# The recurrence of a three-layer kernel: waits taken bank by bank, and another order of its wide products and its sums of returned rows

## The chip, the cores and the metric
The kernel runs on one core of a Trainium2 chip, in one launch. The metric is the device time of the launch in microseconds; the median of three runs counts.

## What is computed
The input x has 4 sequences of 1024 tokens with 256 channels, in fp32. Four layers follow, each on the layer norm of x and added to x: a retention layer, a mixture of experts (8 experts, 2 for each token), the recurrence, and the same experts again. Only the recurrence is touched:
```python
sx = concat([0, x[:, :-1]]) - x                     # the token before, less this one
m = tanh((x + sx * maa_x) @ tm_w1).reshape(B, T, 5, 32)
mix = maa_wkvrg + einsum('btfa,fac->btfc', m, tm_w2)
xw, xk, xv, xr, xg = [x + sx * mix[:, :, i] for i in range(5)]
r, k, v, g = xr @ Wr, xk @ Wk, xv @ Wv, silu(xg @ Wg)
w = exp(-exp(time_decay + tanh(xw @ td_w1) @ td_w2))
# per head of 16 channels, over the tokens, with a = outer(k_t, v_t):
y_t = r_t @ (state + u * a);  state = w_t * state + a
yn = (y - mean(y)) * rsqrt(var(y) + eps) * ln_w + ln_b          # per head
out = (yn * g) @ Wo
```

## The kernel before
Each layer is a block of programs, one for each engine, written out instruction by instruction with semaphores between them; nothing plans the order but these lists. In the recurrence channels lie on the partitions (two halves, kt = 0 and 1) and tokens along the columns. The 4096 tokens are cut into 8 chunks of 512 (n = 0 to 7), two for each sequence. Every engine runs a loop over n that interleaves three chunks: `now` is chunk n, `ahead` chunk n + 1, whose mixes, decays, keys and receptances are made, and `behind` chunk n - 1, whose y is normalised, gated and multiplied with Wo.

Inside a chunk the recurrence is done by blocks of 64 tokens. r and k are multiplied by products of the decays over 2, 4, 8, 16, 32 and 64 tokens (`chain`, 25 steps on DVE); TensorE makes the scores within blocks (`scores_by_4`, `_16`, `_32` for each of four groups i of 128 tokens), DVE masks them (`mask`), `additions` makes what each block of 64 adds to the state, a scan on DVE carries the state (`states`), and `outputs(n, i)` sums scores times v and r times state into y. Near tokens (within 4) are done apart (`near_0`, `near_1_sum`, `near_23_sum`).

PSUM is nearly full: `core` (4 banks) holds scores, y and the additions, and two pairs of banks, `even` and `odd`, are used by all else in turn. So most waits in TensorE's list say that a bank has been read. `mix_scaled` counts DVE's ten mixes of a chunk in the order W_1, W_0, V_0, V_1, K_0, R_0, K_1, R_1, G_0, G_1; each reads one bank of `even` or `odd`. GpSimd then adds x to each (`add_token`, `mix_ready`). `log_ready` counts ACT's logarithm of the variance, which lies in `even`. `hidden_ready` counts two Tanh on ACT that follow the `hiddens` products.

The layer before this one, the experts, leaves its results in DRAM (`y_rows`). For chunk n + 2 they come back by DMA in two tiles, and `add_ys(n + 2, part)` adds them to x on DVE, two instructions for each of four parts; parts 2 and 3 are of the second tile. After part 3 the tiles are free for the next DMA. `stats_of_x` and `moments_of_x` make the statistics of the sum, ACT's `norm` normalises it, and `transpose_x` puts it into `even`.

The lines that matter in the profile: L1909 norm, L1923 tokens, L1930 and L1931 hidden_out, L1942 decay_of, L1949 and L1953 copies of k and r, L1957 copy of v, L1972 silu, L1985 log, L2018 parted copies of r, L2056 y_raw; L2139 is every `linear` (hiddens, hidden_decay, keys, receptances, gate), L2155 deltas, L2188 deltas_g, L2202 decays, L2259 near_0, L2264 near_1_sum and near_23_sum, L2306, L2319 and L2330 the scores by 4, 16 and 32, L2343 transpose_k, L2357 additions, L2378 and L2385 outputs, L2398 variance, L2413 output; L2538 the products of r, L2635 mix, L2671 mask, L2687 the scan, L2738 add_ys; L1833 add_token, L1866 sum_y.

Of the kernel before, what the change touches and what calls it, by code (L numbers as in the profile page):

```python
# [6 lines left out]
ACT = mybir.ActivationFunctionType  # L7
# [6 lines left out]
KT = C // P  # L14
# [1571 lines left out]
CHUNKS = B * CPB  # L1586


def recurrence(nc, held, semaphores, used, d, x, x_stats, y_rows, home, weight, rec_loaded, first_rows, name="rec"):
    with ExitStack() as ctx:  # L1590
# [201 lines left out]
        with nc.Block() as block:  # L1792
# [109 lines left out]
            def _(act):  # L1902
# [80 lines left out]
                def log(c):  # L1983
                    act.wait_ge(var_in_psum, c + 1)
                    act.activation(square[:], even[:], ACT.Ln, bias=eps[:]).then_inc(log_ready, 1)  # L1985

                def root(c):
                    act.wait_ge(log_ready, c + 1)
                    act.activation(square[:], square[:], ACT.Exp, scale=-0.5).then_inc(y_rstd_ready, 1)
# [69 lines left out]
                for n in range(-2, CHUNKS + 1):  # L2059
                    now, ahead, behind = 0 <= n < CHUNKS, 0 <= n + 1 < CHUNKS, n >= 1  # L2060
                    if behind:
                        y_raw(n - 1, 2)
                    if now:
                        k_out(n)
                    if ahead:
# [55 lines left out]
            def _(pe):  # L2121
# [63 lines left out]
                def deltas_g(c):  # L2185
                    pe.wait_ge(hidden_d_ready, c + 1)
                    for kt in range(KT):
                        mm = pe.matmul(odd[:, kt, :], tm_w2_g[LORA * kt:LORA * (kt + 1), kt * P:(kt + 1) * P],  # L2188
                                       hidden_g[LORA * kt:LORA * (kt + 1), :], start=True, stop=True)
                    mm.then_inc(delta_in_psum, 1)  # L2190

                def hidden_decay(c):
                    pe.wait_ge(mix_ready, c * MIXES + W_0)
                    pe.wait_ge(mix_scaled, c * MIXES + R_0)
                    linear(odd[:, 0, :], td_w1, mixed["w"], slice(0, P)).then_inc(d_in_psum, 1)

                def decays(c):
                    pe.wait_ge(hidden_d_ready, c + 1)
                    pe.wait_ge(mix_scaled, c * MIXES + R_1)
                    for kt in range(KT):  # L2200
                        own = slice(kt * LORA_D, (kt + 1) * LORA_D)
                        mm = pe.matmul(even[:, kt, :], td_w2[own, kt * P:(kt + 1) * P], hidden_d[own, :], start=True, stop=True)  # L2202
                    mm.then_inc(decay_in_psum, 1)
# [48 lines left out]
                def near_0(c):  # L2252
                    pe.wait_ge(chain, c * CHAIN + NEAR_0B)
                    if c >= 1:
                        pe.wait_ge(log_ready, c)
                    else:
                        pe.wait_ge(xnt_ready, min(2, CHUNKS))
                    for kt in range(KT):
                        mm = pe.matmul(even[:, kt, :], same_head[:], y_near[:, kt, :], start=True, stop=True)  # L2259
                    mm.then_inc(near_in_psum, 1)  # L2260
# [73 lines left out]
                def transpose_k(c):  # L2334
                    pe.wait_ge(chain, c * CHAIN + K64B)
                    pe.wait_ge(k_copied, c * COPIES + K64_REST)
                    if c + 1 < CHUNKS:
                        pe.wait_ge(mix_scaled, (c + 1) * MIXES + V_0)
                    else:
                        pe.wait_ge(x_added, c)  # L2340
                    for i in range(CT):
                        for kt in range(KT):
                            mm = pe.transpose(even[:, i // 2, i % 2 * C + kt * P:i % 2 * C + (kt + 1) * P],  # L2343
                                              k_64[:, kt, i * P:(i + 1) * P], ident[:])
                    mm.then_inc(k_rows_in_psum, 1)
# [43 lines left out]
                def variance(c):  # L2389
# [7 lines left out]
                    for kt in range(KT):  # L2397
                        mm = pe.matmul(even[:, kt, :], mean_m[:], square[:, kt, :], start=True, stop=True)  # L2398
                    mm.then_inc(var_in_psum, 1)

                def output(c):
# [7 lines left out]
                    else:  # L2409
                        pe.wait_ge(log_ready, c + 1)  # L2410
                    for i in range(CT):
# [13 lines left out]
                for n in range(-2, CHUNKS + 1):  # L2425
# [44 lines left out]
                    if now:  # L2470
                        scores_by_4(n, 3)
                        scores_by_16(n, 3)
                        scores_by_32(n, 3)
                        outputs(n, 1)
                    if ahead:
                        keys(n + 1, 0)
                    if now:
                        outputs(n, 2)
                    if ahead:
                        keys(n + 1, 1)  # L2480
                    if now:
                        outputs(n, 3)
                    if ahead:
                        receptances(n + 1)
                    if now:
                        gate(n, 0)
                        gate(n, 1)
# [4 lines left out]
            def _(dve):  # L2492
# [296 lines left out]
                for n in range(-1, CHUNKS + 1):  # L2789
# [49 lines left out]
                    if now:  # L2839
                        decay_product(n, 32)  # L2840
                        r_to_64(n)
                    if ahead:
                        mix_kr(n + 1, 0)
                    if now:
                        mask(n, 1)
                        states(n)
                    if then:
                        add_ys(n + 2, 2)
                    if ahead:
# [174 lines left out]
```

## Time and profile before

| | us |
|---|---|
| median of 3 runs | 1347.71 |
| lowest, highest | 1342.36, 1349.99 |
| profiled execution, its own time | 1351.96 |
| its span | 1350.1 |
| recurrence, first to last of its instructions in the span | about 555 to 1075 |
| one steady chunk | 58.6 |
| TensorE busy in 59 us of a steady chunk | 54.7 |

An engine's busy time leaves out its waits, so in a chunk of 58.6 us the rest of TensorE's time is waits. A row of the timeline has start, duration, engine, line, operation, out<-in, the count that was merged, and in brackets how long the engine had been idle before it and what released it; "issue" means that nothing in the profile did. Instructions of one engine overlap a little, so a duration reaches into the next row.

### The profile page before, as it was taken

What the parts mean: (1) busy time and instruction counts of PE and PEld (TensorE: products, weight loads), DVE (VectorE), ACT (ScalarE), POOL (GpSimd) and SP (SyncE); (2) the same over time, 40 slices, a digit from 0 to 9 for tenths busy, and PEclk for the clock granted to TensorE, in tenths of its full rate; (3) what the DMA queues carried; (4) which work ended last, traced back from release to release, by engine and by line L of the source; (5) the groups of instructions that cost most, each with busy time, mean ns of one, the idle gap of its engine ahead of it and who ended that gap; (6) DMA issues with size and microseconds to landing.
All of it is one profiled execution on the core that took longest, in us unless ns stands there. A gap on an engine that the chain in (4) does not pass through costs nothing. (4 is left out here: it accounts for less than half of the span.)

```text
span 1350.1 us, 34954 instructions
## 1 busy us (share of the span) xinstructions
PE 1148.6 (85%) x14041; PEld 818.7 (61%) x14041; DVE 927.6 (69%) x1959; ACT 612.8 (45%) x1310; POOL 551.3 (41%) x537
## 2 busy tenths in 40 slices
PE   7999999975699999478999999899987648999970
PEld 4677777763588888235555555555555436888850
DVE  6778787757765655568778797877854376656546
ACT  3344343413355555153736456374653233555534
POOL 3333233202377776325162341516321105777750
PEclk9999999988799999698999999999997679999995
DMA  8132222009643332200000101000000195333338
GB/s 305 55 109 95 88 93 86 35 1 346 209 170 104 104 102 89 72 32 3 33 3 33 33 3 33 4 32 4 2 2 3 33 387 159 104 103 103 105 108 336
DMA packets 50682, 125.66 MB, mean 93 GB/s; under 512 B 7648, under 2 KB 26976, under 8 KB 47712
## 3 DMA queue, kind: packets, MB, share of 16 engines
q1 hardware_dynamic: 36896, 86.20, 17.8%
q0 software_dynamic: 13632, 37.24, 8.8%
q8 instruction: 117, 1.92, 0.6%
q14 instruction: 37, 0.30, 0.1%
HBM read 79.63 MB, written 43.78 MB: 91 GB/s over the span
## 5 line engine op out<-in xcount | busy, mean ns | idle before, releaser
L1090 POOL DMA_INDIRECT ffn_xs<-xn_rows,ffn_from_row x142 | 137.7, 969 | 123.0 <-DVE ffn_second_y_at L1472 80.4
L1098 POOL DMA_INDIRECT y_rows<-ffn_ys,ffn_to_row x142 | 140.2, 987 | 54.9 <-issue 35.2
L1253 PE MATMUL ffn_ps_h<-ffn_w_high,ffn_xst 128*128 x568 | 155.1, 395 | 0.7 <-issue 0.7
L1500 DVE TENSOR_TENSOR ffn_act_in<-ffn_silu_g,ffn_ps_h 128x256 f32<-128x256 f32 x142 | 59.9, 422 | 139.1 <-ACT ffn_silu_g L1132 139.1
L1132 ACT ACTIVATE ffn_silu_g<-ffn_ps_h 128x256 f32<-128x256 f32 x142 | 54.8, 386 | 144.3 <-PE ffn_ps_h L1253 144.3
L1273 PE MATMUL ffn_ps_o<-ffn_w,ffn_act_t 128*128 x284 | 117.2, 435 | 0.5 <-DVE ffn_act_t L1505 0.5
L1253 PEld LDWEIGHTS ffn_ps_h<-ffn_w_high,ffn_xst 128*128 128x128 f32 x568 | 97.3, 190 | 18.2 <-issue 1.2
L1833 POOL TENSOR_TENSOR rec_mixed_w<-rec_mixed_w,rec_xnt 128x512 f32<-128x512 f32 x16 | 17.2, 1090 | 200.0 <-DVE rec_mixed_w L2635 200.0
L1253 PE MATMUL ffn_ps_h<-ffn_w_low,ffn_xst 128*128 x284 | 89.8, 398 | 0.0
L644 DVE TENSOR_TENSOR ret_probs<-ret_score,ret_causal 128x2048 f32<-128x2048 f32 x32 | 73.3, 2292 | 18.2 <-PE ret_score L485 18.2
L1275 PE MATMUL ffn_ps_o<-ffn_w,ffn_act_t 128*128 x284 | 79.2, 279 | 0.0
L292 POOL TENSOR_TENSOR ret_roped<-ret_rope_t 128x512 f32<-128x512 f32 x32 | 40.6, 1270 | 78.6 <-DVE ret_rope_t L637 78.6
L1139 ACT ACTIVATE ffn_ys<-ffn_ps_o 128x256 f32<-128x256 f32 x142 | 54.7, 385 | 29.4 <-PE ffn_ps_o L1275 29.4
L1516 DVE TENSOR_TENSOR ffn_ys<-ffn_ys,ffn_ps_o 128x256 f32<-128x256 f32 x142 | 59.8, 421 | 8.7 <-ACT ffn_ys L1139 2.9
L1148 ACT ACTIVATE ffn_xst<-ffn_ps_t 128x256 fp32r<-128x256 f32 x142 | 55.6, 392 | 16.3 <-PE ffn_ps_t L1243 16.2
L2671 DVE TENSOR_TENSOR rec_probs<-rec_core,home 128x1024 f32<-128x1024 f32 x32 | 39.1, 1221 | 33.2 <-PE rec_core L2385 20.7
L1510 DVE TENSOR_TENSOR ffn_xst<-ffn_ps_t,ffn_xst 128x256 fp32r<-128x256 f32 x142 | 59.0, 415 | 3.4 <-ACT ffn_xst L1148 3.4
L1253 PEld LDWEIGHTS ffn_ps_h<-ffn_w_low,ffn_xst 128*128 128x128 f32 x284 | 53.9, 190 | 11.8
L1505 DVE TENSOR_TENSOR ffn_act_t<-ffn_ps_a,ffn_act_t 128x256 fp32r<-128x256 f32 x142 | 59.4, 418 | 0.8 <-ACT ffn_act_t L1144 0.8
L1243 PE MATMUL ffn_ps_t<-ffn_constants,ffn_xs 128*128 128x128 f32 x284 | 54.8, 275 | 4.9 <-DVE weight L1496 3.3
L1273 PEld LDWEIGHTS ffn_ps_o<-ffn_w,ffn_act_t 128*128 128x128 f32 x284 | 53.6, 189 | 7.3 <-issue 1.1
L1263 PE MATMUL ffn_ps_a<-ffn_constants,ffn_act_in 128*128 128x128 f32 x284 | 54.1, 272 | 0.9 <-DVE ffn_act_t L1505 0.9
(353 smaller groups left out, 2890.2 us busy)
## 6 DMA issues: line engine op xcount, KB each, us to landing
home<-y_rows SPq DMA_DIRECT2D x30, 512.0 KB, 4.8
w_split<-home SPq DMA_DIRECT2D x24, 512.0 KB, 4.3
ffn_w_high<-w_split SPq DMA_DIRECT2D x8, 1024.0 KB, 8.8
ffn_w_low<-w_split SPq DMA_DIRECT2D x8, 1024.0 KB, 10.6
ffn_w<-w_split SPq DMA_DIRECT2D x8, 1024.0 KB, 14.6
home<-in_f_w SPq DMA_DIRECT2D x12, 512.0 KB, 5.8
xn_rows<-home SPq DMA_DIRECT2D x12, 512.0 KB, 11.7
out<-x SPq DMA_DIRECT2D x8, 512.0 KB, 5.7
```

What stands on the lines that cost most here:

```text
L644: dve.tensor_tensor(probs[:].rearrange("p g k h t -> p (g k h) t"), score[:].rearrange("p g (h t) -> p (g h) t", t=P), causal[:].unsqueeze ...
L1090: pool.indirect_dma_start(xs[:, n % SLOTS, :], None, xn_rows[:], bass.IndirectOffsetOnAxis(ap=from_row[:, n:n + 1], axis=0)) \
L1098: pool.indirect_dma_start(y_rows[:], bass.IndirectOffsetOnAxis(ap=to_row[:, m:m + 1], axis=0), ys[:, m % SLOTS, :], None).then_inc(ys_stor ...
L1132: act.activation(silu_g[:, u % 2, :], ps_h[:, u % 2, 0:FF], ACT.Silu).then_inc(silu_ready, 1)
L1148: act.activation(one_pass(xst[:, u % 2, 0]), xt_in_bank(u), ACT.Copy).then_inc(xst_high, 1)
L1253: mm = pe.matmul(ps_h[:, u % 2, :], one_pass(xst[:, u % 2, part, k, :]), one_pass(w1[w_part][k][:, bass.ds(e, E_COLUMNS)]), start=(part + ...
L1273: pe.matmul(ps_o[:, u % 2, :], one_pass(act_t[:, u % 2, 0, k, :]), one_pass(w), start=(k == 0), stop=False)
L1275: mm = pe.matmul(ps_o[:, u % 2, 0:C], one_pass(act_t[:, u % 2, 1, k, :]), one_pass(w[:, 0:C]), start=False, stop=(k == KT - 1))
L1500: dve.tensor_tensor(act_in[:, u % 2, :], silu_g[:, u % 2, :], ps_h[:, u % 2, FF:2 * FF], ALU.mult) \
L1505: dve.tensor_tensor(one_pass(act_t[:, u % 2, 1]), act_t_in_bank, act_t[:, u % 2, 0], ALU.subtract) \
L1510: dve.tensor_tensor(one_pass(xst[:, u % 2, 1]), xt_in_bank(u), xst[:, u % 2, 0], ALU.subtract) \
L1516: dve.tensor_tensor(ys[:, n % SLOTS, :], ys[:, n % SLOTS, :], ps_o[:, u % 2, C:2 * C], ALU.add).then_inc(ys_ready, 1)
```

## The change
ACT's logarithm and TensorE's variance are split by bank, each half with its own count, and the waits on them follow. Four of TensorE's waits on mixes are moved to the mix that read the bank in question (`hidden_decay`, `decays`, `transpose_k`) or added (`deltas_g`). In TensorE's list `keys(n + 1, 0)` goes ahead of `outputs(n, 1)`, `keys(n + 1, 1)` ahead of `outputs(n, 2)`, and `gate(n, 0)` ahead of `outputs(n, 3)`. In ACT's list `k_out(n)` goes ahead of `y_raw(n - 1, 2)`. In DVE's list `add_ys(n + 2, 2)` goes ahead of `mix_kr(n + 1, 0)`.
```diff
 def log(c):
-    act.wait_ge(var_in_psum, c + 1)
-    act.activation(square[:], even[:], ACT.Ln, bias=eps[:]).then_inc(log_ready, 1)
+    for kt in range(KT):
+        act.wait_ge(var_in_psum, c * KT + kt + 1)
+        act.activation(square[:, kt, :], even[:, kt, :], ACT.Ln, bias=eps[:]).then_inc(log_ready, 1)
 def root(c):
-    act.wait_ge(log_ready, c + 1)
+    act.wait_ge(log_ready, (c + 1) * KT)
...
+    if now:
+        k_out(n)
     if behind:
         y_raw(n - 1, 2)
-    if now:
-        k_out(n)
...
 def deltas_g(c):
     pe.wait_ge(hidden_d_ready, c + 1)
+    pe.wait_ge(mix_scaled, c * MIXES + R_0)
 def hidden_decay(c):
     pe.wait_ge(mix_ready, c * MIXES + W_0)
-    pe.wait_ge(mix_scaled, c * MIXES + R_0)
+    pe.wait_ge(mix_scaled, c * MIXES + K_0)
 def decays(c):
     pe.wait_ge(hidden_d_ready, c + 1)
-    pe.wait_ge(mix_scaled, c * MIXES + R_1)
     for kt in range(KT):
+        pe.wait_ge(mix_scaled, c * MIXES + (K_1, R_1)[kt])
...
 def near_0(c):
     pe.wait_ge(chain, c * CHAIN + NEAR_0B)
-    if c >= 1:
-        pe.wait_ge(log_ready, c)
-    else:
+    if c == 0:
         pe.wait_ge(xnt_ready, min(2, CHUNKS))
     for kt in range(KT):
+        if c >= 1:
+            pe.wait_ge(log_ready, (c - 1) * KT + kt + 1)
...
 def transpose_k(c):
-    if c + 1 < CHUNKS:
-        pe.wait_ge(mix_scaled, (c + 1) * MIXES + V_0)
-    else:
+    if c + 1 == CHUNKS:
         pe.wait_ge(x_added, c)
     for i in range(CT):
+        if c + 1 < CHUNKS and i % 2 == 0:
+            pe.wait_ge(mix_scaled, (c + 1) * MIXES + (W_0, V_0)[i // 2])
...
 def variance(c):
     for kt in range(KT):
-        mm = pe.matmul(even[:, kt, :], mean_m[:], square[:, kt, :], start=True, stop=True)
-    mm.then_inc(var_in_psum, 1)
+        pe.matmul(even[:, kt, :], mean_m[:], square[:, kt, :], start=True, stop=True).then_inc(var_in_psum, 1)
...
+    if ahead:
+        keys(n + 1, 0)
+    if now:
         outputs(n, 1)
     if ahead:
-        keys(n + 1, 0)
+        keys(n + 1, 1)
     if now:
         outputs(n, 2)
-    if ahead:
-        keys(n + 1, 1)
-    if now:
+        gate(n, 0)
         outputs(n, 3)
     if ahead:
         receptances(n + 1)
     if now:
-        gate(n, 0)
         gate(n, 1)
...
     if now:
         decay_product(n, 32)
         r_to_64(n)
+    if then:
+        add_ys(n + 2, 2)
     if ahead:
         mix_kr(n + 1, 0)
     if now:
         mask(n, 1)
         states(n)
-    if then:
-        add_ys(n + 2, 2)
     if ahead:
         mix_kr(n + 1, 1)
```
The wait in `output` for the last chunk counts the halves too.

## Rows read from the trace of the kernel before

**Rows 1.** The page, its first part: busy time of each engine.
```profile
PE 1148.6 (85%) x14041; PEld 818.7 (61%) x14041; DVE 927.6 (69%) x1959; ACT 612.8 (45%) x1310; POOL 551.3 (41%) x537
```
**Rows 2.** Windows of two chunks: stretch, length, busy time, clock, DMA.
```profile
763.00:822.00 59.00, 54.59 (x1030) 32.23 (x1029) 47.02 (x78) 33.53 (x50) 20.84 (x18) 1.00 0.06 20
822.00:881.00 59.00, 54.70 (x1031) 32.20 (x1030) 46.94 (x78) 33.46 (x50) 20.74 (x18) 1.00 0.06 21
```
**Rows 3.** The timeline of TensorE's matmuls, 819 to 885 us.
```profile
835.60 1.95 PE L2259 MATMUL rec_even<-rec_y_near,home 128*128 128x512 f32 x4 [0.42 <-ACT rec_square L1985]
...
843.45 1.56 PE L2264 MATMUL rec_odd<-rec_near,home 128*128 128x384 f32 x4
...
849.74 0.64 PE L2330 MATMUL rec_core<-rec_r_32p,rec_k 64*32 64x128 f32 x16 [0.60 <-ACT rec_r_32p L2018]
...
853.90 1.06 PE L2343 MATMUL rec_even<-home,rec_k 128*128 128x128 f32 x8 [0.38 <-DVE rec_mixed_v L2635]
...
858.26 1.95 PE L2139 MATMUL rec_odd<-rec_mixed_w,home 128*128 128x512 f32 x4 [0.46 <-DVE rec_mixed_r L2635]
860.15 0.93 PE L2306 MATMUL rec_core<-rec_r_4p,rec_k 64*64 64x64 f32 x48
...
866.32 1.13 PE L2202 MATMUL rec_even<-rec_hidden_d,home 64*128 64x512 f32 x4 [0.50 <-DVE rec_mixed_r L2635]
867.87 0.93 PE L2306 MATMUL rec_core<-rec_r_4p,rec_k 64*64 64x64 f32 x48 [0.42 <-issue]
...
871.39 0.76 PE L2378 MATMUL rec_core<-rec_probs,rec_v_heads 64*32 64x64 f32 x53 [1.22 <-issue]
```
**Rows 4.** The timeline of ACT in the same stretch.
```profile
832.62 1.02 ACT L1957 ACTIVATE rec_v<-rec_odd 128x1024 f32<-128x1024 f32 x1 [1.29 <-PE rec_odd L2227]
...
834.34 1.11 ACT L1985 ACTIVATE rec_square<-rec_even,rec_eps 128x1024 f32<-128x1024 f32 x1 [0.17 <-PE rec_even L2398]
...
842.72 0.58 ACT L1931 ACTIVATE rec_square<-rec_odd 64x512 f32<-64x512 f32 x1
...
867.66 1.26 ACT L1942 ACTIVATE rec_w<-rec_even,home 128x512 f32<-128x512 f32 x2
```
**Rows 5.** The timeline of DVE in the same stretch.
```profile
834.22 0.88 DVE L2738 SCALAR_TENSOR_TENSOR x<-home,weight,x 128x256 f32<-128x256 f32 x2 [0.42 <-DMA home<-y_rows]
...
854.49 0.68 DVE L2538 TENSOR_TENSOR rec_r<-rec_r,rec_w 128x512 f32<-128x512 f32 x1
856.71 0.75 DVE L2635 SCALAR_TENSOR_TENSOR rec_mixed_k<-rec_odd,home,rec_sx 128x512 f32<-128x512 f32 x1 [1.53 <-PE rec_odd L2155]
...
862.11 2.74 DVE L2738 SCALAR_TENSOR_TENSOR x<-home,weight,x 128x256 f32<-128x256 f32 x2
...
868.54 2.10 DVE L2738 SCALAR_TENSOR_TENSOR x<-home,weight,x 128x256 f32<-128x256 f32 x2
```
**Rows 6.** The timeline of GpSimd in the same stretch.
```profile
854.50 2.67 POOL L1833 TENSOR_TENSOR rec_mixed_v<-rec_mixed_v,rec_xnt 128x512 f32<-128x512 f32 x2
```
**Rows 7.** The DMA view of 868 to 873 us: GB/s in 40 slices, then the queue.
```profile
GB/s 0 0 0 0 0 0 0 0 0 131 0 0 0 0 0 0 0 0 0 0 0 0 0 0 0 0 0 0 0 0 0 0 0 0 0 0 131 0 0 0
```
**Rows 8.** Waits of the outputs, 600 to 1000 us, and four such rows of TensorE's timeline.
```profile
PE rec_core L2378 <- issue: 4.8, 7, 1.2
...
PE rec_core L2385 <- issue: 1.7, 2, 0.8
...
695.41 0.40 PE L2385 MATMUL rec_core<-rec_r,rec_state 32*32 32x64 f32 x10 [0.84 <-issue]
...
740.98 0.28 PE L2357 MATMUL rec_core<-rec_v,rec_silu_g 64*32 64x32 f32 x12 [1.40 <-issue]
741.20 3.59 PE L2139 MATMUL rec_odd<-rec_mixed_w,home 128*128 128x512 f32 x4
...
986.97 0.35 PE L2385 MATMUL rec_core<-rec_r,rec_state 32*32 32x64 f32 x7 [0.82 <-issue]
```
**Rows 9.** Two windows behind the wait at 740.98; columns as in rows 2.
```profile
741.00:743.00 2.00, 2.00 (x15) 0.93 (x15) 1.61 (x3) 0.00 (x0) 2.00 (x3) 0.61 0.00 0
743.00:745.00 2.00, 2.00 (x19) 0.50 (x21) 1.97 (x2) 0.18 (x1) 1.92 (x2) 0.54 0.03 8
```
**Rows 10.** The timeline of the last chunk.
```profile
1054.10 6.05 PE L2139 MATMUL rec_odd<-rec_mixed_g,home 128*128 128x512 f32 x8
...
1060.81 1.28 ACT L2076 ACT_TABLE_LOAD   x1
```

More of the change, by code:

```diff
@@ L2409, in output @@
                     else:
-                        pe.wait_ge(log_ready, c + 1)
+                        pe.wait_ge(log_ready, (c + 1) * KT)
                     for i in range(CT):
@@ L2473, in _ @@
                         scores_by_32(n, 3)
-                        outputs(n, 1)
                     if ahead:
@@ L2477, in _ @@
                     if now:
-                        outputs(n, 2)
+                        outputs(n, 1)
                     if ahead:
@@ L2481, in _ @@
                     if now:
+                        outputs(n, 2)
+                        gate(n, 0)
                         outputs(n, 3)
```

## The prediction, on record before the change was run

> **What bounds the kernel now.** I read the page first: TensorE is busy for 85% of the span, DVE for 69% [rows 1]. Only the recurrence is changed, so the table of windows came next, one window per chunk of 512 tokens: in a steady chunk of 59 us TensorE is busy for about 54.7 us, DVE for 47, ACT for 33.5 and GpSimd for 21, at a granted clock of 1.00, the 2.4 GHz level [rows 2]. So TensorE has some 4 us of waits in a chunk, and only those can be won. The timeline of TensorE in the chunk of 822 to 881 us names them [rows 3]: 0.42 us before `near_0`, 0.60 before `scores_by_32(0)`, 0.38 before `transpose_k`, 0.46 before `hidden_decay`, 0.50 before `decays`, 0.42 before `scores_by_4(3)`, and 1.22 inside `outputs(1)`, which nothing in the profile releases ("issue"). The timelines of ACT, DVE and GpSimd [rows 4 to 6] show what each of these waits hangs on. The reader is to see two stretches in them. In the first, ACT works without a break from the copy of v at 832.62 to the last copy of r at 849.6, and TensorE waits for it at the end of that. In the second, from 849.7 to 867.9, the order runs from mask to mixes to state to sums to mixes to mask on DVE, and TensorE waits several times for it. After 867.9 TensorE runs by itself up to the next v.
>
> All times below are those of this one chunk. The sum is made against the profiled execution, 1351.96 us (span 1350.1), which is 4.25 us above the median of the three runs, 1347.71; a difference worked out in it is taken off the median. A run of this kernel can tell about 0.5%, 6.7 us, from no change.
>
> **Logarithm by bank (first stretch).** `near_0` now waits for half of the logarithm, so its 0.42 us before 835.60 goes [rows 3]. But what is late next is `near_23_sum`, at 843.45 straight behind the score matmuls: it waits for `hidden_ready`, whose second Tanh starts at 842.72 and ends at 843.30 [rows 4]. And `scores_by_32(0)` still waits for the last copy of r. Both ends hang on ACT's chain, which starts with v at 832.62 [rows 4]. The split itself: one Ln of 1114 ns waited 0.17 us for TensorE [rows 4]; the nearest pair of halves is the Exp of the decays, two in 1.26 us, where one of full width takes 1.06, so 0.2 us more, of which 0.17 comes back as the first half needn't wait for the second variance matmul. Zero, with bounds of -0.2 and +0.2 us a chunk. `var_in_psum` on each matmul adds no instruction.
>
> **Waits by bank on the mixes (second stretch).** `transpose_k` starts behind W_0 rather than V_0: its first four transposes run while DVE scales v. It starts at 853.52, when the 16-wide scores end, instead of 853.90: 0.38 us. `deltas_kr_0` ends 0.38 earlier too, at 856.2. `hidden_decay` needs K_0 and not R_0, so the 0.46 us before it can go. The added wait in `deltas_g` (R_0) is long met. The second wait in `decays` lets the first matmul start one mix earlier, and costs nothing by itself.
>
> **Sums of returned rows ahead of `mix_kr(0)`.** Before, `add_ys(n+2, 2)` follows the scan: 2.74 us at 862.11 [rows 5], and the mixes K_1 and R_1 and mask(2) queue behind it, for which `decays`, `y_raw(0)` and `scores_by_4(3)` wait. Now it starts when `r_to_64` ends, at 855.17, where DVE sat idle for 1.53 us before K_0 at 856.71 [rows 5]. Its price there isn't seen. With GpSimd idle the pair takes 0.88 us (834.22); with GpSimd adding it took 2.10 (868.54) and 2.74 [rows 5]. GpSimd adds v from 854.50 to 857.17 [rows 6], the operation that it also ran at 868.54, so I take 2.10. Then:
> - K_0 starts at 857.27 instead of 856.71 (0.56 later) and ends at 858.0; `hidden_decay` starts at 858.1 instead of 858.26.
> - mask(1), the state and `scores_by_4(2)` are 0.56 later: 860.71 instead of 860.15 [rows 3]. From there `outputs(0)` ends 4.6 us later as before, at 865.3.
> - K_1 and R_1 no longer queue behind the sums: they start with the end of `deltas_kr_1`, at 863.65, and end at 865.0, under `outputs(0)`. mask(2) starts at 865.4, when `outputs(0)` is done. Before, it started after 2.74 of sums and 1.32 of mixes, at 866.1.
> - TensorE goes on without a wait: `deltas_g` 865.25, `decays` 866.3, `scores_by_4(3)` 867.37 instead of 867.87 [rows 3].
> So 0.50 us a chunk. With 0.88 for the pair K_0 starts at 856.33, all is 0.38 earlier than before, and `scores_by_4(3)`, then behind `decays`, starts at 866.43: 1.44 us. With 2.74 it starts at 868.01, a loss of 0.14. There are six such chunks (n = 0 to 5): 6 x 0.50 = 3.0 us, between -0.8 and 8.6. Chunk 6 has no sums and keeps the 0.38: 0.4 us.
>
> The GPSIMD Engine Reference of the Trainium skill (Key points) says that GpSimd shares its SBUF interfaces with VectorE and is in each other's way with DVE instructions that have two SBUF inputs. These sums have two, and the rows agree (0.88 against 2.10 and 2.74). By that rule the price of 0.88 falls away, since GpSimd works at the new place; the sum by it is the one that I take, and without it the other.
>
> **Wide products between outputs (after 867.9).** Call U the start of `scores_by_4(3)`. Scores and outputs issue 192 matmuls and weight loads each in 1.9 and 1.5 us, back to back, and in the middle of that stands a wait of 1.22 us with no releaser [rows 3]. The DMA view of that stretch has one 16 KB transfer of the instruction queue just before it, from about 869.1, and the next when TensorE moves again [rows 7]; nothing else is on the DMA. I read it as TensorE's program arriving late. Outputs waited in that way nine times between 600 and 1000 us, 6.5 us in all [rows 8]; five of these, in chunks 1, 2, 3, 4 and 6, stand in `outputs(1)` and are 0.84, 0.60, 1.06, 1.22 and 0.82, together 4.5 us (the first and the last in [rows 8]). In the new order `keys(0)`, 16 instructions over 2 us, lie between the third scores and `outputs(1)`, `keys(1)` and `gate(0)` between the others. I take it that all 4.5 us go; bounds none and all.
>
> What the order costs: `keys(0)` needs decay_out, there by U + 1.1. `outputs(2)` waits for mask(3) and `y_raw(1)`, covered by `keys(1)` as before by `keys(0)`. `y_raw(2)` now queues behind a table load (1.28 us) and the copy of k, to U + 9.8; `gate(0)` covers that up to U + 10.5. The copy of r starts at U + 15.65, then the square and the two Silu: the last ends at U + 18.65, while the transposes of x end at U + 18.4. `values` waits for it, some 0.35 us in each of seven chunks: 2.4 us. DVE's first products start at most 1.4 us later after a chunk without a stall, and it had 0.84 us before sx and 0.42 at the DMA of the returned rows to spare, so its end is the same. Hence 4.5 - 2.4 = 2.1 us, between -2.4 and 4.5.
>
> The Runtime page of the Trainium skill (NRT & Kernel Launch, Instruction fetch mechanics) says that the next 16 KB page is fetched while this one runs and that the fetch is mostly hidden by the pace of issue. If so, the gaps are something else and the new order takes none away; the transfer just ahead of the gap [rows 7] speaks for the fetch.
>
> **The last chunk.** `gate(0)` ahead of `outputs(3)` holds back the last y. Before, the gates took 6.05 us from 1054.10, against 3.6 us in a steady chunk, and the second Silu and a table load at 1060.81 came last before the logarithm [rows 10]. Now y is up to 2.8 us later, but two Silu and the table load stand between the square and the logarithm, and the load, tied to the end of the gates, is still what comes last. -0.3 us, between 0 and -1.3.
>
> Sum: 3.0 + 0.4 + 0 + 2.1 - 0.3 = 5.2 us. 1347.7 - 5.2 = **1342.5 us**.
>
> **The rivals.**
> - *The sums are nearly free* (0.88 a pair, as at 834.22). For: the pairs at the place of 834.22 have it in every chunk, and DVE has 1.53 us free. Against: GpSimd works there. 6 x 1.44 instead of 3.0: 10.8 us, 1336.9. The same comes if the stalls at `outputs(0)` go too and the waits shrink further.
> - *The stalls only move.* For: the program stays as long, and a gap of the same kind (1.40 us) stood in `additions` at 740.98 [rows 8]. Then 5.2 - 4.5 = 0.7 us: 1347.0.
> - *Slower.* The place is the wait before `hidden_decay`. If a pair of sums costs 3.1 us (twice 1.55, the longest of one), K_0 ends at 859.0, TensorE idles 1.6 us before it and `scores_by_4(3)` is 0.5 us late against before: +3.0. After the idle 1.40 us at 740.98 the clock was granted at 0.54 to 0.61 and `hidden_decay` took 3.59 us instead of 1.95 [rows 3, 8, 9]: 1.64 us more. In six chunks that is 9.8. With the other terms (-0.4 - 2.1 + 0.3) it gives +10.6: 1358.3. It decides from about 2.6 us a pair, where the second stretch gives nothing. Against: none of the pairs beside the same addition took more than 2.11.
>
> **How the numbers follow.** Chances: my forecast 0.44 (by its own bounds 1339.5 to 1345), the nearly free sums 0.23, the stalls that move 0.21, slower 0.12. Faster by over 0.5% means below 1341.0: the second case and the lower part of the first, 0.23 + 0.17 = 0.40. Slower by over 0.5%: 0.11. Between: 0.49. The range runs from 1335 to 1349, from a little below the nearly free sums to above the moved stalls, and leaves out the slower case.
>
> **What would show it.** No wait before `near_0`, but one before `near_23_sum`, with `scores_by_32(0)` still about 0.6 us behind ACT. The pair of sums before K_0 at 2.1 us, and K_1 straight behind `deltas_kr_1`. No gap without a releaser in `outputs(1)` to `outputs(3)`. `values` waiting for Silu by 0.3 us. The distance of one copy of r to the next falls from 58.6 us to about 57.7. I am wrong if the clock falls in the second stretch, or if gaps appear in `additions` or `outputs(0)` as long as those that go.

## The result and the profile after

In 20 runs of each, side by side, the changed kernel had a median of 1344.84 us and the kernel before 1349.74 us; the ratio is 0.9962, with a 95% interval of 0.9946 to 0.9978. That is 0.38% or 5.1 us, by the interval 3.0 to 7.3 us, where the prediction had 5.2 us. On another chip (`r_after` below) the ratio was 0.9976 (0.9950 to 1.0002). By the bound of 0.5% this is no change that a measurement of three runs tells; 20 runs tell it.

Two chunks in the windows of the changed kernel, columns as in [rows 2], where TensorE was busy for 54.6 and 54.7 us:
```profile
763.00:822.00 59.00, 55.84 (x1034) 32.57 (x1033) 46.23 (x78) 33.21 (x49) 22.60 (x21) 1.00 0.06 20
822.00:881.00 59.00, 55.81 (x1033) 32.47 (x1032) 46.66 (x79) 34.82 (x51) 20.75 (x18) 1.00 0.06 20
```
TensorE has lost one of its four microseconds of waits. The timeline of its matmuls in the chunk that answers to [rows 3]:
```profile
825.16 3.69 PE L2229 MATMUL rec_odd<-home,rec_mixed_v 128*128 128x256 f32 x16 [0.53 <-ACT rec_silu_g L1972]
...
831.28 1.88 PE L2261 MATMUL rec_even<-rec_y_near,home 128*128 128x512 f32 x4
...
838.73 0.93 PE L2308 MATMUL rec_core<-rec_r_4p,rec_k 64*64 64x64 f32 x48 [0.39 <-ACT rec_k L1993]
...
845.87 0.64 PE L2332 MATMUL rec_core<-rec_r_32p,rec_k 64*32 64x128 f32 x16 [0.61 <-ACT rec_r_32p L2019]
...
849.59 1.09 PE L2345 MATMUL rec_even<-home,rec_k 128*128 128x128 f32 x8
...
854.58 1.96 PE L2140 MATMUL rec_odd<-rec_mixed_w,home 128*128 128x512 f32 x4 [1.05 <-DVE rec_mixed_k L2636]
856.98 0.93 PE L2308 MATMUL rec_core<-rec_r_4p,rec_k 64*64 64x64 f32 x48 [0.45 <-issue]
...
862.66 1.13 PE L2204 MATMUL rec_even<-rec_hidden_d,home 64*128 64x512 f32 x4
863.72 0.93 PE L2308 MATMUL rec_core<-rec_r_4p,rec_k 64*64 64x64 f32 x48
...
867.39 0.86 PE L2380 MATMUL rec_core<-rec_probs,rec_v_heads 64*32 64x64 f32 x64
```
The waits before `near_0`, `transpose_k`, `decays` and `scores_by_4(3)` are gone, and `outputs(n, 1)` at 867.39 runs through. Four others are there: 0.39 us before `scores_by_4(0)`, among the near sums, 1.05 us before `hidden_decay` (0.46 in the kernel before), 0.45 us before `scores_by_4(2)`, which starts 0.1 us after DVE has masked what `additions` made, and 0.53 us before `values`. DVE in the same chunk, against [rows 5]:
```profile
851.23 2.54 DVE L2739 SCALAR_TENSOR_TENSOR x<-home,weight,x 128x256 f32<-128x256 f32 x2
853.69 0.74 DVE L2636 SCALAR_TENSOR_TENSOR rec_mixed_k<-rec_odd,home,rec_sx 128x512 f32<-128x512 f32 x1
...
856.91 1.75 DVE L2688 TENSOR_TENSOR_SCAN rec_state<-rec_s_mult,rec_s_add 128x576 f32<-128x576 f32 x1
859.99 0.75 DVE L2636 SCALAR_TENSOR_TENSOR rec_mixed_k<-rec_even,home,rec_sx 128x512 f32<-128x512 f32 x1 [1.32 <-PE rec_even L2156]
...
861.78 1.22 DVE L2672 TENSOR_TENSOR rec_probs<-rec_core,home 128x1024 f32<-128x1024 f32 x1 [0.38 <-PE rec_core L2387]
```
The pair of sums sits ahead of K_0 and takes 2.54 us, and K_1 follows `deltas_kr_1` as forecast.

For what follows I cut each chunk into three stretches, by start times in the timelines: (a) from the copy of v to `scores_by_32(0)`, (b) from there to `scores_by_4(3)`, (c) from there to the next copy of v. The table gives their sums over chunks 0 to 6, (b) of chunk 4 alone, and the time in which TensorE was granted 1.2 GHz within these seven chunks. A profile is one execution; ratios are to the kernel before on the same chip. Chunks 1, 3, 4 and 5 are called steady; chunk 2 has a wait of 1.40 us in `additions` [rows 8], with the clock at 1.2 GHz behind it.

| kernel | a | b | c | sum | b, chunk 4 | at 1.2 GHz | ratio (95%) |
|---|---|---|---|---|---|---|---|
| before | 119.3 | 129.5 | 160.3 | 409.1 | 18.13 | 10.2 | |
| changed | 118.5 | 128.6 | 157.9 | 405.0 | 17.85 | 10.2 | 0.9962 (0.9946 to 0.9978) |
| `r_after`, the same again | 118.5 | 134.3 | 160.0 | 412.8 | 17.51 | 23.9 | 0.9976 (0.9950 to 1.0002) |
| `e1_order` | 119.3 | 128.7 | 158.4 | 406.4 | 18.14 | 6.8 | 0.9981 (0.9950 to 1.0011) |
| `e2_sums` | 119.3 | 131.0 | 160.0 | 410.2 | 17.64 | 13.7 | 0.9987 (0.9962 to 1.0011) |
| `e3_banks` | 118.8 | 124.3 | 160.3 | 403.4 | 17.14 | 6.8 | 0.9930 (0.9901 to 0.9958) |
| `e4_no_sums` | 118.4 | 129.9 | 158.9 | 407.3 | 17.13 | 20.5 | 0.9947 (0.9919 to 0.9974) |
| `e5_late_sums` | 118.8 | 123.0 | 158.5 | 400.3 | 16.86 | 6.8 | 0.9932 (0.9906 to 0.9959) |
| `e6_late_silu` | 120.5 | 128.5 | 155.3 | 404.3 | 17.25 | 17.1 | 0.9912 (0.9878 to 0.9946) |
| `e7_pad` | 119.3 | 129.5 | 160.5 | 409.2 | 18.15 | 10.2 | 1.0072 (1.0048 to 1.0096) |
| `e8_pad128` | 119.3 | 127.1 | 164.5 | 410.9 | 18.13 | 10.2 | 0.9986 (0.9964 to 1.0009) |
| `e9_padded` | 120.5 | 127.0 | 156.7 | 404.2 | 19.28 | 17.1 | 0.9948 (0.9927 to 0.9969) |
| `e10_transposes` | 119.3 | 124.5 | 160.8 | 404.6 | 17.12 | 10.2 | 0.9969 (0.9948 to 0.9991) |
| `e11_decays` | 119.3 | 130.6 | 161.0 | 410.8 | 18.14 | 10.2 | 1.0045 (1.0019 to 1.0070) |

The profiled execution of the changed kernel has a span 9.8 us below that of before. Of this, 4.1 us are the seven chunks, 1.5 us lie ahead of the first copy of v and 1.1 us in the last layer, which the change doesn't touch, and 3.1 us in the last chunk (66.4 us from its copy of v to the last layer, instead of 69.5). The other kernels of the table have 63.4 to 68.0 us there with either order, so I put none of the 3.1 down to the change. What makes up the rest between the 4.1 us of the chunks and the 5.1 us of the times is not shown.

### The profile page after: what moved, and what is told of

The parts are those of the page before. It is cut to its first block and busy times, and to the rows that moved or that the text cites. A ratio compares the mean times of both kernels' runs of the same rounds, so it can differ in the third digit from the quotient of the medians.

```text
span 1340.3 us, 34970 instructions
## 1 busy us (share of the span) xinstructions
PE 1143.6 (85%) x14041; PEld 811.6 (61%) x14041; DVE 924.4 (69%) x1959; ACT 612.4 (46%) x1318; POOL 552.7 (41%) x537
## 5 line engine op out<-in xcount | busy, mean ns | idle before, releaser
L1139 ACT ACTIVATE ffn_ys<-ffn_ps_o 128x256 f32<-128x256 f32 x142 | 54.6, 384 | 28.5 <-PE ffn_ps_o L1275 28.5
L1243 PE MATMUL ffn_ps_t<-ffn_constants,ffn_xs 128*128 128x128 f32 x284 | 54.6, 274 | 3.3 <-DMA ffn_xs<-xn_rows,ffn_from_row 1.9
L2140 PE MATMUL rec_odd<-rec_mixed_w,home 128*128 128x512 f32 (+1 forms) x96 | 50.7, 660 | 7.2 <-DVE rec_mixed_k L2636 5.9
```

What stands on the lines that cost most here:

```text
L1243: mm = pe.transpose(ps_t[:, u % 2, k * P:(k + 1) * P], xs[:, n % SLOTS, k * P:(k + 1) * P], ident[:])
```

## The experiments

### The three parts of the change alone
`e1_order`: the kernel before with the new order of wide products, and `k_out` ahead of `y_raw(n - 1, 2)`, and nothing else.
```diff
+    if ahead:
+        keys(n + 1, 0)
+    if now:
         outputs(n, 1)
     if ahead:
-        keys(n + 1, 0)
+        keys(n + 1, 1)
...
+        gate(n, 0)
         outputs(n, 3)
```


> Before with the new order of wide products and of the copy of k alone. Theory: the gaps without a releaser in outputs(n, 1) are TensorE's program arriving late at a 256-instruction page; with keys between they go (4.5 us over chunks 1 to 6) and values waits 0.35 to 0.5 us for Silu in seven chunks. From scores_by_4(3) to the next copy of v: 160.3 us over seven chunks before, 157.9 now; the other two stretches as before; ratio 0.998. Rival: the gaps stem from something in outputs itself and stay: then the stretch grows to about 163 and the ratio is 1.002.


Stretch (c) takes 158.4 us, 1.9 less, and (a) and (b) of the steady chunks are as before. The view of who waited for whom, TensorE, 600 to 1000 us (waited for: us, times, longest), against [rows 8]:
```profile
PE rec_odd L2227 <- ACT rec_silu_g L1972: 4.6, 7, 1.4
...
PE rec_core L2378 <- issue: 1.9, 5, 0.6
```
Outputs waited 1.9 us without a releaser instead of 6.5, and no such wait is left in `outputs(n, 1)`: those that are left stand in `outputs(n, 0)`. `values` waits 4.6 us for Silu. The rival, that the gaps stay, falls. The ratio, 0.9981, can't be told from 1.

`e2_sums`: the kernel before with the sums moved and nothing else.
```diff
+    if then:
+        add_ys(n + 2, 2)
     if ahead:
         mix_kr(n + 1, 0)
...
     if now:
         mask(n, 1)
         states(n)
-    if then:
-        add_ys(n + 2, 2)
```


> Before with the sums of part 2 ahead of the mixes K_0 and R_0 alone. From the profile of the changed kernel the pair costs 2.6 us at the new place (1.31 each beside GpSimd's sums of v), not 2.10. Theory: K_0 comes 1.1 us later, and hidden_decay, which here still waits for R_0, too; from scores_by_32(0) to scores_by_4(3) the chunks 1, 3, 4, 5 go from 18.13 to between 18.1 and 18.6; ratio 1.000 to 1.002. Rival, my prediction's step: 0.5 us less a chunk, 17.6, ratio 0.998.


Neither alone. Chunks 3 and 4 take 17.63 and 17.64 us in (b), just what my prediction's step had (0.5 less), though the pair costs 2.54 us: the scan is 1.75 us long instead of 2.24 and gives the 0.4 back. Chunks 1 and 5 take 18.31 and 18.18, with waits of 0.56 and 0.28 us without a releaser in `outputs(0)`, to which the section on the sums' place comes back. Chunk 0 shows what the prediction named as a sign of being wrong, a fall of the clock in this stretch: TensorE is granted 1.2 GHz from 632.2 to 635.6 us, behind a wait of 0.98 us before `hidden_decay`, and the stretch takes 23.3 us instead of 20.2. The ratio, 0.9987, can't be told from 1.

`e3_banks`: the changed kernel without the new order and without the moved sums, so the waits by bank alone.

> Before with the waits by bank alone (logarithm, mixes, decays, transposes of k). Theory: from v to scores_by_32(0) 17.11 goes to 16.98 as in the changed kernel; from there to scores_by_4(3) the 0.38 us of transpose_k is passed on to the end: 18.13 to 17.75; together 0.5 us a chunk, 3.5 us, ratio 0.997. Rival: the sums behind the scan hide it and nothing but 0.13 is left: 0.9 us, ratio 0.999.


Far more than either: (b) is 17.13 us in each steady chunk, 1.0 less, and the ratio 0.9930. By the median this part alone is faster than the whole change (0.9962), and its seven chunks take 403.4 us against 405.0; the intervals of the ratios overlap a little, 0.9946 to 0.9958.

### Which wait by bank
`e10_transposes` and `e11_decays` split the waits of stretch (b): the kernel before with only the first of these edits, or only the second.
```diff
 def transpose_k(c):
...
     for i in range(CT):
+        if c + 1 < CHUNKS and i % 2 == 0:
+            pe.wait_ge(mix_scaled, (c + 1) * MIXES + (W_0, V_0)[i // 2])
```
```diff
 def deltas_g(c):
     pe.wait_ge(hidden_d_ready, c + 1)
+    pe.wait_ge(mix_scaled, c * MIXES + R_0)
...
 def hidden_decay(c):
...
-    pe.wait_ge(mix_scaled, c * MIXES + R_0)
+    pe.wait_ge(mix_scaled, c * MIXES + K_0)
...
 def decays(c):
...
-    pe.wait_ge(mix_scaled, c * MIXES + R_1)
     for kt in range(KT):
+        pe.wait_ge(mix_scaled, c * MIXES + (K_1, R_1)[kt])
```


> Before with the waits by bank of transpose_k alone. All three waits together (e3) took the stretch from scores_by_32(0) to scores_by_4(3) from 18.14 to 17.13 us, of which transpose_k's 0.38 was forecast; in e3 the scan took 1.61 us instead of 2.23. Theory: the earlier transposes alone bring K_0 0.38 earlier, the scan then lies otherwise against GpSimd's sums and is 0.6 us shorter: 17.13 here too, ratio 0.996. Rival: the other 0.6 comes from hidden_decay, which needn't wait for R_0: 17.75 here, ratio 0.998.

> Before with the waits of hidden_decay, decays and deltas_g alone. Theory: hidden_decay starts 0.46 us earlier, but the end of the stretch hangs on DVE's mixes and the scan: 18.1 us as before, ratio 1.000. Rival: 17.5 or less, ratio 0.997.


The transposes alone give all of the 1.0 us of stretch (b), 17.12 us in a steady chunk; the other waits nothing, 18.14. How 0.38 us became 1.0 stands in the timeline of DVE in `e10_transposes` (this chunk's `scores_by_32(0)` starts at 895.8):
```profile
902.36 0.75 DVE L2635 SCALAR_TENSOR_TENSOR rec_mixed_k<-rec_odd,home,rec_sx 128x512 f32<-128x512 f32 x1 [1.12 <-PE rec_odd L2155]
...
905.60 1.59 DVE L2687 TENSOR_TENSOR_SCAN rec_state<-rec_s_mult,rec_s_add 128x576 f32<-128x576 f32 x1
907.12 2.79 DVE L2738 SCALAR_TENSOR_TENSOR x<-home,weight,x 128x256 f32<-128x256 f32 x2
```
and in that of GpSimd:
```profile
904.89 1.09 POOL L1833 TENSOR_TENSOR rec_mixed_k<-rec_mixed_k,rec_xnt 128x512 f32<-128x512 f32 x1
905.94 2.14 POOL L1833 TENSOR_TENSOR rec_mixed_r<-rec_mixed_r,rec_xnt 128x512 f32<-128x512 f32 x1
908.04 1.59 POOL L1856 TENSOR_TENSOR rec_y_near<-rec_y_near,rec_near 128x512 f32<-128x512 f32 x1
```
Before, the same two engines:
```profile
859.95 2.23 DVE L2687 TENSOR_TENSOR_SCAN rec_state<-rec_s_mult,rec_s_add 128x576 f32<-128x576 f32 x1
```
```profile
859.88 1.08 POOL L1833 TENSOR_TENSOR rec_mixed_r<-rec_mixed_r,rec_xnt 128x512 f32<-128x512 f32 x1
860.93 2.44 POOL L1856 TENSOR_TENSOR rec_y_near<-rec_y_near,rec_near 128x512 f32<-128x512 f32 x1
```
In `e10_transposes` the scan starts 0.34 us before GpSimd's sum of r and takes 1.59 us, and that sum is stretched to 2.14. Before, it started 0.07 us after it, took 2.23, and the sum its normal 1.08. So 0.4 us of shift go with 0.64 us of scan. In the last chunk, with no such sums on GpSimd, the scan took 1.36 us.

The 112 scans of the 14 traces show who is served first. The sum that GpSimd had begun when the scan started kept its usual time (1.1 us for r or k), and the scan took 1.36 us and what was left of that sum, less 0.14: 1.49 us with 0.27 left (`e6_late_silu`), 1.60 with 0.38 (`e10_transposes`), 1.75 with 0.54 (the changed kernel), 2.23 with 1.01 (before), 2.58 with 1.36 (`r_after`). All 97 scans with over 0.1 us left fit this within 0.01 us, and where GpSimd's sum of r began behind the scan, it was the sum that took longer, 2.14 to 2.20 us.

In `e11_decays` the seven chunks are 1.7 us longer: a wait of 2.00 us without a releaser stands in the third scores of chunk 3, where the kernel before has none. The rest of its 1.0045 (0.45% slower, clear of noise) I can't place.

### The sums' place
`e4_no_sums`: the changed kernel with part 2 of the sums back behind the scan. `e5_late_sums`: part 2 behind the mixes of g instead, right ahead of part 3:
```diff
     if ahead:
         mix_g(n + 1)
     if then:
+        add_ys(n + 2, 2)
         add_ys(n + 2, 3)
```


> The changed kernel with the sums of part 2 back behind the scan. In the changed kernel the pair takes 2.62 us ahead of K_0, and scores_by_32(0) to scores_by_4(3) takes 18.00, 17.49, 17.85 and 18.26 us in chunks 1, 3, 4, 5. Theory: the move of the sums gives nothing; here the stretch takes 17.75 (18.13 less the 0.38 of transpose_k) and the time is that of the changed kernel within 1 us. Rival, my prediction's step: 17.75 here against 17.5 or less with the move, this kernel 2 to 3 us slower than the changed one.

> The changed kernel with the sums of part 2 moved behind the mixes of g, beside those of part 3, where DVE waits 2.0 us for mask(3). Theory: the pair is in the way wherever it stands between mask(0) and mask(2); taken out, K_0 starts 1.3 us earlier, deltas_kr_1, outputs(0), deltas_g and decays follow without a wait and scores_by_4(3) starts 16.7 us after scores_by_32(0) instead of 17.5 to 18.3: some 1.1 us in six chunks, 6.5 us below the changed kernel, ratio to before 0.991. Rival: mask(3) comes late instead, as the sums of both parts run beside GpSimd's sums of g (2.1 us a pair), and the stretch after scores_by_4(3) grows from 22.6 by as much as is won.


With the sums back, (b) is 17.10, 17.13 and 17.14 us in chunks 1, 4 and 5, against 18.00, 17.85 and 18.26 in the changed kernel: with the move these chunks take 0.7 to 1.1 us longer once the transposes start early.

Not all of that is the price of the sums. From its first matmul to its last `outputs(0)` takes 1.29 us, and more where a wait without a releaser stands in it. With the sums behind the scan DVE doesn't wait for `outputs(0)` before mask(2) in these chunks, so this costs nothing: in chunks 1, 4 and 5 of `e4_no_sums` `outputs(0)` takes 1.94, 2.19 and 1.79 us, and (b) is the same. With the sums moved DVE does wait for it, as the row of the changed kernel at 861.78 shows. The second half of `outputs(0)` in chunks 3 and 4 of the changed kernel, the one without such a wait and the one with it:
```profile
803.53 0.72 PE L2387 MATMUL rec_core<-rec_r,rec_state 32*32 32x64 f32 x32
...
860.59 1.08 PE L2387 MATMUL rec_core<-rec_r,rec_state 32*32 32x64 f32 x32
```
In chunk 3, where nothing was late there, (b) is 17.49, and so it is in chunk 4 of `r_after`, 17.51: 0.4 us above 17.13. In chunks 1, 4 and 5 of the changed kernel `outputs(0)` takes 0.38, 0.36 and 0.78 us more than in chunk 3, and (b) 0.51, 0.36 and 0.77. In `e2_sums` it is the same: 0.69 and 0.56 us more in chunks 1 and 5 for `outputs(0)`, 0.67 and 0.54 for (b).

In chunk 3 `e4_no_sums` had 22.2 us, with TensorE at 1.2 GHz, so its sum is no measure; its ratio, 0.9947, lies below that of `r_after` on the same chip, 0.9976, but the intervals overlap. Behind the mixes of g, (b) is 17.02, 16.41, 16.86 and 16.89 us in chunks 1, 3, 4 and 5. DVE in chunk 3 of `e5_late_sums`:
```profile
795.99 0.75 DVE L2636 SCALAR_TENSOR_TENSOR rec_mixed_k<-rec_odd,home,rec_sx 128x512 f32<-128x512 f32 x1 [1.12 <-PE rec_odd L2156]
...
806.40 3.28 DVE L2739 SCALAR_TENSOR_TENSOR x<-home,weight,x 128x256 f32<-128x256 f32 x4
...
811.27 1.22 DVE L2672 TENSOR_TENSOR rec_probs<-rec_core,home 128x1024 f32<-128x1024 f32 x1 [0.93 <-PE rec_core L2387]
```
All four sums take 3.28 us there and mask(3) still waits 0.93 us for `outputs(n, 1)`, so they are covered. The median is 1342.85 us against 1349.2 for `r_after` on the same chip, 6.4 us less where 6.5 were expected; but the profile of `r_after` lost 5 us of this to the clock, and the intervals overlap a little. The rival, mask(3) late, falls: (c) is 22.5 to 22.9 us as with the changed kernel.

### Silu ahead of the copy of r
`e6_late_silu` is `e5_late_sums` with ACT's list changed: `silu(n - 1, 0)` stands ahead of `r_out(n)`.

> e5 with the first Silu ahead of the copy of r on ACT, where ACT waits 3 us. Theory: values waits no more for Silu (0.53 us in the changed kernel), from the copy of r to that of v 6.82 goes to 6.3 in seven chunks: 3.5 us below e5. Rival: the transposes of x, which wait for the copy of r, and the table load set the end: nothing.


Less than half. (c) falls from 22.5 to 22.0 us in most chunks, but (a) grows from 16.98 to 17.31, so that some 0.15 us a chunk are left. In ACT's timeline the copy of k_8's rest is what is late next:
```profile
831.40 1.02 ACT L1957 ACTIVATE rec_v<-rec_odd 128x1024 f32<-128x1024 f32 x1 [1.30 <-PE rec_odd L2230]
832.65 0.63 ACT L1993 ACTIVATE rec_k<-rec_k 128x512 f32<-128x512 f32 x1 [0.23 <-DVE rec_k L2543]
```
The copy of r comes no earlier, and DVE, which works from it without a break, now sets ACT's start. The ratio, 0.9912, is the lowest of all, with the interval of 0.9878 to 0.9946; whether the Silu's move adds to `e5_late_sums` (0.9932) isn't settled.

### The gaps without a releaser
`e7_pad` and `e8_pad128` add tiny matmuls at the start of the recurrence, and are otherwise the kernel before. The lines are those of `e8_pad128`; `e7_pad` has 64 of them, all on one tile of 32x32. `e9_padded` is `e6_late_silu` with the same addition as `e8_pad128`.
```diff
 keep_going(odd[:, 1, :], 14)
+for i in range(32):
+    own = slice(i % 4 * 32, i % 4 * 32 + 32)
+    pe.matmul(odd[own, 1, 0:64], ident[own, 0:32], ident[own, 0:64], start=True, stop=True)
```


> Before with 64 tiny matmuls more (128 instructions with their weight loads, 32x32 by 64 columns, on results that are overwritten) at the start of the recurrence, in hiddens(0). If the gaps are late pages of TensorE's program, each gap without a releaser is again at the same place of the count modulo 256 (193 with matmuls and weight loads counted from the start of the program), so 128 instructions earlier or later in the work: not one of the old gaps stays at its matmul, and their sum changes. Rival: a wait that belongs to the outputs: the gaps stay at the same matmul of outputs(n, 1), which is then 128 further on in the count. Time: same as before within 3 us in both.

> Before with 32 tiny matmuls more at the start of the recurrence, spread over four quadrants. An fp32 matmul is two matmuls and two weight loads in the records, so this is 128 instructions, half a page (the 64 matmuls of e7_pad were 256, a whole page, and its gaps lay at the same matmuls as before). If the gaps are late pages of TensorE's program, all of them keep the place 193 in the count modulo 256 and so stand 128 instructions away from the old ones in the work: none at its old matmul. Rival, a wait that belongs to the outputs: same matmul, the count shifts by 128 and is 65 modulo 256. Time: within 5 us of before in both, plus some 1 us for the added matmuls.


Counting every record of TensorE in the trace from the start of the program, its matmuls and weight loads and also its semaphore waits and register operations, these gaps of over 0.5 us without a releaser came out, with the time of the instruction behind each:
```
before     count  mod 256   us      gap    e8_pad128  count  mod 256   us      gap
           11457    193    630.73  0.59               11969    193    681.03  1.70
           14017    193    695.41  0.84               14017    193    740.62  1.14
           15297    193    740.98  1.40               16065    193    799.43  2.02
           16065    193    754.51  0.60               20417    193    916.46  0.92
           18113    193    812.87  1.06               22465    193    974.77  1.31
           20161    193    871.39  1.22               24513    193   1031.55  1.07
           21953    193    923.26  0.83               26561    193   1087.98  0.56
           24513    193    986.97  0.82
```
All stand at the same place modulo 256, and so do those of the other 12 traces in their seven chunks. (The expectation of `e7_pad` names matmuls and weight loads alone. Counted so, the first three gaps of the kernel before are at 222, 173 and 145 modulo 256: the other instructions belong to the program too.) In `e7_pad` my 64 matmuls were 256 instructions in the records (an fp32 matmul is two, each with a weight load), a whole page of 256: the gaps came at 14273, 15553, 16321, 18369 and 20417, which is 256 further on and thus at the same matmuls, so that run told nothing apart. With 128 they kept the 193 and moved in the work. The gap in `outputs(1)` of chunk 1, in the timeline of `e8_pad128`:
```profile
739.07 0.42 PE L2381 MATMUL rec_core<-rec_probs,rec_v_heads 64*32 64x64 f32 x22
740.62 0.66 PE L2381 MATMUL rec_core<-rec_probs,rec_v_heads 64*32 64x64 f32 x42 [1.14 <-issue]
```
It stands behind 22 matmuls of `outputs(1)`. Before it stood behind 86, at 695.41 [rows 8]: 64 matmuls and their 64 loads earlier. So the gaps belong to TensorE's program, read 256 instructions at a time, and to no operation. The DMA records say the same: the instruction queue has one transfer of 16 KB for each 256 records (57 of both between 600 and 1000 us in the kernel before), and in all 14 traces each of these gaps in the seven chunks ends 1.2 to 1.6 us behind the end of such a transfer. `e7_pad` was slow because its matmuls, all on one tile, took 13.9 us one behind the other; the chunks themselves took 409.2 us as before. The four kernels from `e8_pad128` to `e11_decays` in the table ran on a chip where the kernel before had 1437 us, while the seven chunks took as long as elsewhere; their ratios are to that.

> e6 with the same 128 instructions. In e6 the largest gaps stood in additions and the third scores (1.33 us in chunk 2, 2.27 in chunk 3), and the clock fell behind the second for 6.8 us. If pages set them, they stand elsewhere now, where keys and gates give time; without a fall of the clock the stretch from scores_by_32(0) to scores_by_4(3) of chunk 3 goes from 21.6 to 16.9 us and the time is 3 to 5 us below e6's. Rival: the same number and length of gaps at other places, time as e6.


The gaps moved and didn't go: 1.90 us at the count of 16065 (chunk 2), 1.66 at 19649, 1.46 at 21697. Chunk 3 has its 16.90 us in (b), but chunks 4 and 5 now have 19.28 and 19.41. The sum, 404.2 us, is that of `e6_late_silu`, 404.3: the rival holds.

### The changed kernel again


> The changed kernel once more, on the same chip as the three beside it: ratio to before 0.996, stretches as in its first profile within 0.1 us except where a page of TensorE's program or the clock falls otherwise.


The ratio, 0.9976 where 0.996 was expected, fits within its interval; the profile doesn't: (b) of chunk 3 took 22.45 us. Windows of that stretch:
```profile
807.00:809.50 2.50, 0.50 (x27) 0.29 (x13) 0.50 (x1) 0.00 (x0) 2.42 (x2) 1.00 0.00 0
809.50:815.00 5.50, 5.50 (x117) 2.75 (x109) 2.64 (x3) 0.35 (x1) 2.43 (x3) 0.61 0.01 3
815.00:821.00 6.00, 6.00 (x103) 3.44 (x102) 4.09 (x6) 2.36 (x4) 2.32 (x2) 0.50 0.01 3
```
TensorE waits 1.99 us for a page at 807.30, the clock is granted at 0.61 and then 0.50, and the chunk loses 5 us. The same happened in chunk 3 of `e4_no_sums` and `e6_late_silu`, behind waits of 1.72 and 2.27 us.

## Why the prediction came out right, step by step

**The total, 5.2 us: right, and in part by luck.** For the seven chunks I had forecast 5.5 us (0 in the first stretch, 3.4 in the second, 2.1 behind `scores_by_4(3)`); the profile has 4.1 (0.8, 0.9 and 2.4). The largest term came out at about a quarter of its size and two smaller ones came out higher. That the time fell by 5.1 us, so close to 5.2, owes something to chance: the chunks show 4.1, and the interval is 3.0 to 7.3. The rivals fall with the time and with the rows: the pair of sums took 2.54 us and not 0.88 (10.8 us forecast), and the gaps didn't only move (0.7 us forecast), they fell from 7.8 to 3.0 us.

**Logarithm by bank: 0 forecast, 0.13 us a chunk measured** (17.11 to 16.98 in stretch (a), 0.8 us in all), within the bounds. The 0.42 us before `near_0` came back as 0.39 before the first scores, and TensorE still waited 0.61 for the last copy of r. The two Ln took 1.26 us, as the pair of Exp. The size held; the place didn't: I had `near_23_sum` waiting next, for `hidden_ready`, but it waits for nothing, and `scores_by_4(0)` waits for a copy of k.

**Waits by bank on the mixes: mis-sized.** I passed on the 0.38 us of `transpose_k` and no more. It is worth 1.0 us a chunk (`e10_transposes`, `e3_banks`), because the scan is 0.6 us shorter when it starts a little earlier against GpSimd's sums: 0.38 us of the sum of k were left instead of 1.01 of the sum of r. I had passed the scan on at one length whatever it met. `hidden_decay` and `decays` were rightly put at nothing.

**Sums ahead of `mix_kr(0)`: the place and the chain were right, the price too low, and its sign wrong beside the other part.** The pair costs 2.54 us rather than 2.10. Relative to `scores_by_32(0)`, K_0 started at 7.82 us (forecast 7.53), `scores_by_4(2)` at 11.11 (10.97), mask(2) at 15.91 (15.66), `scores_by_4(3)` at 17.85 (17.63). So 0.28 us were gained in this chunk where 0.50 were forecast. The dearer pair takes 0.44 us of the 0.50, and the scan, 1.75 us instead of 2.23, gives that back; what is missing is in the main a late page in `outputs(0)`, which took 0.36 us more than in chunk 3, where 0.65 us were gained. I had the end of `outputs(0)` set the start of mask(2), and let it run as before, without asking what would then come of late pages in it. Nor did I ask what the chunk would take with the waits by bank and without this move: 17.13 us. Beside them the move takes back 0.4 us by itself and, with the late pages that it lays open, 0.7 to 1.1. The forecast for (b), 3.4 us, became 0.9: chunks 1 and 5 gained 0.14 and lost 0.14, and chunk 0 lost 0.9.

**Wide products between outputs: right.** 2.1 us forecast, 2.4 measured (160.3 to 157.9), 1.9 by itself in `e1_order`. Pages that come late cost the kernel before 7.8 us in these chunks and the changed one 3.0; `values` pays 0.53 us a chunk for Silu, where I had 0.35. The Runtime page of the Trainium skill (NRT & Kernel Launch, Instruction fetch mechanics) says that this fetch is mostly hidden by the pace of issue. By the rows it isn't hidden where scores and outputs follow each other, with 0.6 to 2.3 us shown for one page, and the measurement decides. The shortest page of the kernel before took 2.9 us from its first instruction to that of the next, 0.60 us of wait included. One reading of mine was off: the transfer behind the gap at 871.39 starts 1.2 us after TensorE moves again, and not with it [rows 7].

**The last chunk: not settled.** -0.3 us forecast; the profiles of both orders scatter by 4.6 us there, with TensorE at 1.2 GHz for 17 to 27 us of it (34 in the kernel before).

**Slower: didn't come.** The idle time before `hidden_decay` is 1.05 us, not 1.6, and the clock stayed at 1.00 behind it in the steady chunks. In the seven chunks the clock fell in two places, as before: in chunk 0 behind a wait of 2.87 us for the last copy of r, and in chunk 2 behind a late page of 1.33 us.

## What to carry to other kernels
Price a moved instruction against the kernel in which all the other edits already stand: here two edits that each took time off the same chain were worth less together than one alone. Where a small shift changes which of two engines starts first, as with the scan and GpSimd's sum of r, the change is larger than the shift, and a split experiment finds it where the sum of durations doesn't. An edit that takes one engine off the critical path lays open the waits of the next: ask what those were. Dense runs of small matmuls waited here for their own program; put wide products between them, and count all of the engine's instructions modulo 256 before blaming an operation.

## What the runs showed of the hardware that I had not expected
- A scan of 128x576 on DVE took 1.36 us with GpSimd idle, and otherwise 1.36 us and what was left of the sum that GpSimd had begun before it, less 0.14, up to 2.58; the sum of r of 128x512 that began behind the scan took 2.14 to 2.20 us instead of 1.08. Of these two, the one that starts first is served first. A pair of sums of 128x256 on DVE took 0.88 us alone and 2.1 to 2.8 beside GpSimd.
- TensorE's waits of over 0.5 us without a releaser lie at one place in 256 of its instructions and last up to 2.3 us (`e6_late_silu`), each ending 1.2 to 1.6 us behind the end of a 16 KB transfer on the instruction queue.
- Behind some of them the clock falls to the 1.2 GHz level (1.33 us in the changed kernel) and behind others it doesn't (1.94 us in `e3_banks`); two profiles of one kernel had it for 10.2 and 23.9 us in the seven chunks. An effect of 0.3% can be read from the stretches of steady chunks and hardly from one run's time.
- 64 matmuls of 32x32 by 64 columns in fp32 on one tile took 13.9 us (`e7_pad`), and 32 of them over four tiles 1.6 us (`e8_pad128`): 217 and 52 ns each, with the clock granted at 0.50 and 0.61.
- The best version here is `e6_late_silu` at 0.9912 (0.9878 to 0.9946), 0.6% below the changed kernel's 0.9976 (0.9950 to 1.0002) on the same chip; it has the new order of products, the waits by bank, the sums behind the mixes of g, and the Silu's move, whose share isn't settled.
